# Explicit 4x4 inverses with TensorE sums, key dimension outermost, half roots and TensorE-made gated weights in a gated delta-rule block

## The chip, the cores and the metric

The kernel runs on one core of one Trainium2 chip. The metric is the time of one execution on the device, in microseconds (us), from the start of the program to its end. Everything is computed in float32.

## The reference

A block with adaptive layer norms: an attention part with a recurrent state (a gated delta rule), then a feed-forward part in which each row goes to one of 8 experts. The batch is 16, the length 256, the width 128, with 16 heads of 8 dimensions.

```python
h = _layernorm(x) * (1 + ca) + sa            # sa, ca, ga, sb, cb, gb from silu(c) @ wmod
q, k = silu(h @ Wq), silu(h @ Wk); v = h @ Wv            # per head, 8 dimensions
k = k * rsqrt(sum(k * k, -1) + 1e-12)
beta = 2.0 * sigmoid(h @ Wbet); a = sigmoid(h @ Wf)
def step(S, inp):                            # 256 steps, S is 8x8 for each batch row and head
    Sd = a * S
    u = v - einsum('bhk,bhkv->bhv', k, Sd)
    Sn = Sd + beta * k[..., None] * u[:, :, None, :]
    return Sn, einsum('bhk,bhkv->bhv', q, Sn)
o = o * rsqrt(mean(o * o, -1) + 1e-6)
x = x + ga * ((o.reshape(b, n, d) * norm_w) @ Wo)
h = _layernorm(x) * (1 + cb) + sb
x = x + gb * experts(h)                      # argmax of 8, silu(a) * g @ w2, times the top probability
```

## The kernel before, in words

The 128 partitions hold 8 batch rows times 16 heads, so the recurrence has two halves h = 0 and 1 (8 batch rows each). Time is cut into chunks of C = 4 steps: there are 64 chunks, n = 0 to 63. The first 128 steps (chunks 0 to 31) are slice 0, the others slice 1. A group g is four chunks.

Inside a chunk the four steps are coupled by a lower-triangular 4x4 matrix (tile L, one for each chunk, from the products of unit keys, decays and beta). Solving with it is forward substitution, `substitute(h, s, j)` for j = 0, 1, 2: a product of a column of L with a row of X (written to TMP), then a subtraction from the rows below it. VectorE does both. For slice 0 this is done ahead of the loop. For slice 1 it is done in the gaps of the loop.

VectorE runs the loop over the chunks. Each chunk has four steps for each half: `from_state` (L1476), `sum_u` (L1482), `outer` (L1489), `next_state` (L1495). After each of these eight instructions VectorE takes one piece of a second list of work, `next(other)`. That list is `second_preparation` (slice 1: key norms, unit keys, decay factors, key products, substitution), then `first_slice_rows` (gated output weights, sums of squares, roots, second layer norm and routing of slice 0). `after_chunk(n)` holds the list back until chunk n is done; the constants `PREP`, `SOLVE`, `AT_WOG`, `AT_ROOT` and so on are such chunks. `settle` gives up the turn after an instruction whose result is needed by the next piece.

ScalarE follows the same chunks with a fixed order written in a loop over n. In each round it first copies `ubar` (if n is even), scales the state (`decay`, L1060, which `next_state` of the same chunk waits for), stages keys every fourth chunk (`stage`), keeps states (`keep_states`, L1074), evacuates finished outputs from PSUM (`out_group`, L1090, at the chunks of `OUT_AT`), then does single jobs such as `query_evac` (L1028, at the chunks of `QK_AT`).

GpSimd makes the products of queries with states and of weights with U for each group and half (`make_products`, L280 and L287, into two alternating slots of prod_o), and in between the products of slice 1: `multiply_keys` (L833), `weigh_keys` (L799), `multiply_queries` (L824), `decay_keys` (L810), `decay_queries` (L841, L846). TensorE sums these products with an identity as weights and accumulates in PSUM: `sum_outputs` (L570, L574), `sum_queries` (L589), `sum_keys` (L602). `make_products` waits until the slot's last sum is done, and `sum_outputs` waits until the bank has been evacuated by `out_group`. For queries and keys the products lie with the key dimension k innermost (8 floats), so TensorE reads every eighth float.

A reciprocal root is made in three parts. VectorE adds the epsilon (L1347, L1306, L1504), ScalarE takes `Sqrt` (`root`, L944), and VectorE takes the reciprocal (L1354, L1287) and refines it by one Newton step.

The gated output weights WOG[b] = norm_w * Wo * gate[b] are made by TensorE and VectorE: TensorE spreads the gate of row b over the partitions (`gate_columns`, L557), then VectorE multiplies it by NW and WO (`weigh_columns`, L1449, sixteen instructions in chunks 32 to 35).

After the loop the last outputs are squared, summed, scaled (L239), moved by DMA, multiplied by WOG (`attend`, L618), and the feed-forward part follows: tiles of 128 rows, 46 of them, each on TensorE with the weights of one expert (L715, L730).

## Time and profile before

| | |
|---|---|
| median of 3 runs | 510.71 us (509.48 to 512.72) |
| the profiled execution | 512.15 us, of which 510.4 us are the span of the profile |
| busy in the span | PE 372.3, PEld 309.3, DVE 415.1, ACT 272.7, POOL 276.6 us |
| mean granted TensorE clock | 0.873 |

PE is TensorE's matmuls and PEld its weight loads, DVE is VectorE, ACT is ScalarE, POOL is GpSimd. The rows give the start of an instruction from the start of the span. An fp32 matmul stands as two records. In a row of the timeline, neighbouring instructions of one line are merged (x4), and the idle time in front of them stands in brackets with what ended it. The recorded durations of VectorE overlap a little: of two that follow each other directly, the second starts some 0.08 us before the first one's recorded end. What one costs the others is therefore the distance between starts.

### The profile page before, as it was taken

To read this page: it belongs to the slowest core of one execution; us is meant where nothing else is said; L and a number is where in the kernel's file an instruction comes from. 1 tells how busy PE (TensorE), PEld (TensorE's weight loads), DVE (VectorE), ACT (ScalarE), POOL (GpSimd) and SP (SyncE) were. 2 spreads that over 40 slices of the span, in tenths; PEclk is the share of its full clock that TensorE was granted. 3 is DMA by queue.
4 is the path that set the end of the run, shared out by engine and by line. 5 is a ranking of instruction groups with operands and counts; after the bars stand their busy time and mean duration, and the time that the engine had idled before them with its cause. 6 is when DMAs were issued, how large, how long until landed. Compare 5 with 4: busy or idle time off the path is not lost. (4 is left out here: it accounts for less than half of the span.)

```text
span 510.4 us, 8398 instructions
## 1 busy us (share of the span) xinstructions
PE 372.3 (73%) x2387; PEld 309.3 (61%) x2387; DVE 415.1 (81%) x1196; ACT 272.7 (53%) x600; POOL 276.6 (54%) x323
## 2 busy tenths in 40 slices
PE   2855861959928789843296876585999998999970
PEld 1312220426526658843296766585989997999970
DVE  4759999999999999999999899966595743559734
ACT  2587876957225225464556546273375566655520
POOL 1166244889999959641838828601132277633340
PEclk9996786888869799777598977799899999999995
DMA  8185788990000002910400000114313013424006
GB/s 218 45 89 98 89 115 131 141 71 2 0 0 2 0 0 81 368 49 0 75 10 2 0 1 32 54 36 76 76 39 105 31 54 105 130 59 133 29 26 170
DMA packets 50203, 34.98 MB, mean 69 GB/s; under 512 B 10992, under 2 KB 46608, under 8 KB 50032
## 3 DMA queue, kind: packets, MB, share of 16 engines
q1 hardware_dynamic: 47152, 29.07, 29.4%
q0 software_dynamic: 3008, 5.40, 3.5%
q8 instruction: 20, 0.33, 0.3%
q14 instruction: 23, 0.19, 0.2%
HBM read 15.26 MB, written 10.27 MB: 50 GB/s over the span
## 5 line engine op out<-in xcount | busy, mean ns | idle before, releaser
L570 PE MATMUL bank<-prod_o,ID 128*128 128x128 f32 x512 | 80.6, 323 | 43.1 <-POOL prod_o L287 21.7
L570 PEld LDWEIGHTS bank<-prod_o,ID 128*128 128x128 f32 x512 | 75.3, 233 | 48.0 <-POOL prod_o L287 24.6
L918 POOL DMA_INDIRECT placed_y<-Q,place x46 | 44.1, 958 | 98.6 <-ACT Q L1223 56.2
L715 PE MATMUL bank<-Q,p 128*128 128x128 f32 x736 | 95.0, 277 | 0.0
L715 PEld LDWEIGHTS bank<-Q,p 128*128 128x128 f32 x736 | 89.9, 193 | 0.1
L1060 ACT ACTIVATE p<-S,GAM 128x64 f32<-128x64 f32 x126 | 48.4, 409 | 75.9 <-DVE S L1495 75.2
L280 POOL TENSOR_TENSOR prod_o<-Q,ST 128x1024 f32<-128x1024 f32 x28 | 61.9, 2211 | 37.3 <-PE bank L574 26.2
L1216 ACT ACTIVATE p<-big 128x1024 f32 x46 | 48.5, 1057 | 44.3 <-PE bank L715 41.7
L1495 DVE TENSOR_REDUCE S<-p 128x64 f32<-128x320 f32 x126 | 55.1, 471 | 0.8 <-ACT p L1060 0.8
L1482 DVE TENSOR_REDUCE U<-p 128x32 f32<-128x288 f32 x128 | 52.4, 437 | 0.0
L1476 DVE TENSOR_TENSOR p<-S,bank 128x256 f32<-128x256 f32 x128 | 49.0, 405 | 0.7 <-ACT bank L1055 0.7
L1489 DVE TENSOR_TENSOR p<-U,bank 128x256 f32<-128x256 f32 x126 | 47.1, 405 | 0.0
L537 PE MATMUL bank<-ph,WP 128*128 128x512 f32 x48 | 32.1, 823 | 18.8 <-ACT ph L956 12.7
L287 POOL TENSOR_TENSOR prod_o<-PD,U 128x128 f32<-128x128 f32 (+1 forms) x112 | 42.5, 415 | 0.0
L865 POOL DMA_INDIRECT sorted_h<-X,pos x32 | 30.8, 964 | 14.1 <-issue 8.5
L1685 DVE COPY Q<-bank 128x128 f32<-128x128 f32 x46 | 13.2, 287 | 28.7 <-PE bank L703 28.6
L730 PE MATMUL bank<-big,S 128*128 x248 | 33.3, 277 | 2.0 <-DVE Q L1699 2.0
L574 PEld LDWEIGHTS bank<-prod_o,ID 128*128 128x128 f32 x256 | 34.3, 208 | 0.0
L574 PE MATMUL bank<-prod_o,ID 128*128 128x128 f32 (+3 forms) x256 | 33.8, 279 | 0.0
L1692 DVE TENSOR_TENSOR S<-S,bank 128x512 f32<-128x512 f32 x31 | 21.2, 685 | 15.4 <-PE bank L715 14.4
L730 PEld LDWEIGHTS bank<-big,S 128*128 128x128 f32 x248 | 30.1, 192 | 2.8 <-issue 2.8
L537 PEld LDWEIGHTS bank<-ph,WP 128*128 128x128 f32 x48 | 11.4, 254 | 33.0 <-issue 16.2
(225 smaller groups left out, 747.5 us busy)
## 6 DMA issues: line engine op xcount, KB each, us to landing
big<-in_L_ffn_w_dram SPq DMA_DIRECT2D x1, 4096.0 KB, 13.4
big<-big SPq DMA_DIRECT2D x16, 192.0 KB, 4.7
Q<-sorted_h SPq DMA_DIRECT2D x46, 64.5 KB, 2.1
sorted_h<-ZERO SPq DMA_DIRECT2D x2, 1472.0 KB, 16.3
X<-in_L_attn_x_dram SPq DMA_DIRECT2D x8, 256.0 KB, 4.5
big<-big SPq DMA_DIRECT2D x16, 128.0 KB, 5.1
X<-Q SPq DMA_DIRECT2D x32, 64.0 KB, 2.4
K<-placed_y SPq DMA_DIRECT2D x8, 256.0 KB, 3.5
```

The costliest lines, as they stand in the source:

```text
L280: engine.tensor_tensor(slot[:, 0:HD, :, :, :], q, states.unsqueeze(3).broadcast_to(full), ALU.mult)
L570: pe.matmul(ps, ID[:, :], prod_o[:, k % 2, i, :], start=(i == 0), stop=False, skip_group_check=True)
L574: m = pe.matmul(o4, ID[:, :], r4, start=False, stop=(d == C - 1), skip_group_check=True)
L715: m = pe.matmul(bank[(1, 6)[g % 2] + k][:, c * P:(c + 1) * P], W1E[g % 2][:, f:f + P], XST[:, g % 3, :], start=True, stop=True)
L730: m = pe.matmul(bank[3][:, 0:D], GU[g % 3][:, c * P:(c + 1) * P], W2[:, bass.ds(expert, 1), c, :], start=(c == 0), stop=(c == FC - 1))
L918: pool.indirect_dma_start(placed_y[g // NF], bass.IndirectOffsetOnAxis(ap=place[:, g:g + 1], axis=0), YS[:, g % YR, :], None).then_inc(sem ...
L1060: act.activation(p2[h][:, :, :, C], S_[h][:, n % SR, :, :], ACT.Copy, scale=GAM[h][:, n:n + 1])\
L1216: act.activation(W1E[g % 2].unsqueeze(1), W1[:, bass.ds(expert, 1), :], ACT.Copy).then_inc(sem("w1_copied"), 1)
L1476: dve.tensor_tensor(p1[h][:, n % UR, :, :, 0:HD], s_, w, ALU.mult).then_inc(sem("seq_w", h), 1)
L1482: dve.tensor_reduce(U_[h][:, n % VR, :, :], p1[h][:, n % UR, :, :, :], AX_X, ALU.add)\
L1489: dve.tensor_tensor(p2[h][:, :, :, 0:C], u, k, ALU.mult).then_inc(sem("state_in", h), 1)
L1495: dve.tensor_reduce(S_[h][:, (n + 1) % SR, :, :], p2[h][:, :, :, :], AX_X, ALU.add).then_inc(sem("s_ready", h), 1)
```

## The change

It has five parts.

- Slice 1, half 0: the three pairs of product and subtraction are replaced by `invert(0)` (six small VectorE instructions that turn L into the inverse's entries) and `multiply_solved(0)` (the three products with the untouched X, without subtractions). TensorE sums row i and its i products in bank 0 (`solve(0, i)`), ScalarE copies the sum back to X (`solved(0, i)`, at chunks 19, 23 and 24 for i = 3, 2, 1). Half 1 is still solved by substitution.
- The products of queries and keys lie with k outermost: GpSimd writes with a step of 320 or 192 floats between neighbouring k, and TensorE reads contiguous columns.
- Roots: ScalarE takes `Abs_reciprocal_sqrt` of 4x + 4 eps, so it gives half of the reciprocal root, and VectorE does three instructions. The epsilon instruction, the reciprocal and (for the keys) a copy are gone. The operands of two of the three are now both in SBUF also for the keys. An early `Sqrt` of ScalarE after the loop is gone.
- Gated weights: TensorE transposes Wo and the gates once (`turn_weights`), ScalarE makes sixteen diagonal matrices (two in each of chunks 15 to 22, `spread_gates`), TensorE multiplies (`weigh_columns`, 16 matmuls in front of group 6), and ScalarE scales by norm_w while it copies (`scale_columns`, chunks 31 to 34). VectorE's sixteen instructions are gone.
- `OUT_AT` of group 4 goes from chunks 25, 25 to 26, 27, and of group 5 from 27, 28 to 28, 29. In TensorE's order, `solve(0, 3)` stands after the sums of group 2, and `solve(0, 2)` and `solve(0, 1)` after those of group 3, in front of the last `sum_queries`. Some waits are moved to other semaphores.

```diff
+    SOLVED = (C, 2)
+    SOLVE_AT = {(2, 1): (3,), (3, 1): (2, 1)}
+    SOLVED_AT = {19: 3, 23: 2, 24: 1}
-    OUT_AT = {..., 4: (25, 25), 5: (27, 28), 6: (30, 31), ...
+    OUT_AT = {..., 4: (26, 27), 5: (28, 29), 6: (30, 31), ...
...
+        def by_dimension(region, pairs):
+            return region[:, 0:pairs * HD].rearrange("p (k x) -> p k x", k=HD)
-                    m = pe.matmul(..., ID[:, :], terms[:, :, k], ...)
+                    m = pe.matmul(..., ID[:, :], query_terms(j)[:, k, :], ...)
...
+            def solve(h, i):
+                if i == C - 1:
+                    pe.wait_ge(sem("solved_terms"), h + 1)
+                else:
+                    pe.wait_ge(sem("prep_done", h), C - 1 - i + 1)
+                pe.matmul(solved_sum(h), ID[:, :], solved_row(h, i), start=True, stop=False)
+                for j in range(i):
+                    m = pe.matmul(solved_sum(h), ID[:, :], solved_products(h, j)[:, :, i - j - 1, :], ...)
+                m.then_inc(sem("solved_ps"), 1)
+            def weigh_columns():
...
+                    m = pe.matmul(bank[(5, 0, 1, 4)[b // 4]][...], WO[:, :], WOG[:, b, :], start=True, stop=True)
...
                     sum_outputs(g, h)
+                    for i in SOLVE_AT.get((g, h), ()):
+                        solve(0, i)
...
-                act.activation(dst, src, ACT.Sqrt).then_inc(sem("root_out"), 1)
+                act.activation(half, src, ACT.Abs_reciprocal_sqrt, scale=4.0, bias=4.0 * eps).then_inc(sem("root_out"), 1)
...
+            def solved(h, i):
+                act.wait_ge(sem("solved_ps"), (C - 1) * h + C - i)
+                act.activation(solved_row(h, i), solved_sum(h), ACT.Copy).then_inc(sem("prep_done", h), 1)
...
-            act.activation(sd[:, :], ve[:, :], ACT.Sqrt)
...
-                yield from settle(dve.reciprocal(y, sroot))
-                yield from settle(dve.tensor_tensor(t, y, y, ALU.mult))
-                yield from settle(dve.scalar_tensor_tensor(out=t, in0=t, scalar=-0.5, in1=var, op0=ALU.mult, op1=ALU.mult))
-                dve.scalar_tensor_tensor(out=y, in0=t, scalar=1.5, in1=y, op0=ALU.add, op1=ALU.mult)...
+                yield from settle(dve.scalar_tensor_tensor(out=t, in0=half, scalar=-4.0, in1=half, op0=ALU.mult, op1=ALU.mult))
+                yield from settle(dve.scalar_tensor_tensor(out=t, in0=var, scalar=eps, in1=t, op0=ALU.add, op1=ALU.mult))
+                dve.scalar_tensor_tensor(out=y, in0=t, scalar=3.0, in1=half, op0=ALU.add, op1=ALU.mult)...
...
+            def invert(h):
+                yield from settle(dve.tensor_tensor(two, pair(2, 1, 2), pair(1, 0, 2), ALU.mult))
+                yield from settle(dve.tensor_tensor(one, pair(3, 1), pair(1, 0), ALU.mult))
+                yield from settle(dve.tensor_tensor(pair(2, 0, 2), pair(2, 0, 2), two, ALU.add))
+                yield from settle(dve.tensor_tensor(other_, pair(3, 2), pair(2, 0), ALU.mult))
+                yield from settle(dve.tensor_tensor(one, one, other_, ALU.add))
+                yield from settle(dve.tensor_tensor(pair(3, 0), pair(3, 0), one, ALU.add))
+            def multiply_solved(h):
+                for j in range(C - 1):
...
+                    last = dve.tensor_tensor(solved_products(h, j), col..., X4[:, :, j:j + 1, :]..., ALU.mult)
...
             def second_preparation():
...
-                yield from substitute(0, 1, 0)
+                yield from invert(0)
+                yield from multiply_solved(0)
                 yield from unit_keys(1, 1)
                 yield
-                for j in (1, 2):
-                    yield from substitute(0, 1, j)
             def first_slice_rows():
-                for q in range(4):
-                    yield from after_chunk(AT_WOG + q)
-                    yield from weigh_columns(q)
```

## Rows read from the trace of the kernel before

**Rows 1.** Page, part 1: busy time, share of the span, instructions.

```profile
PE 372.3 (73%) x2387; PEld 309.3 (61%) x2387; DVE 415.1 (81%) x1196; ACT 272.7 (53%) x600; POOL 276.6 (54%) x323
```

**Rows 2.** Windows: busy time of PE, PEld, DVE, ACT, POOL in a stretch, granted clock.

```profile
129.00:149.00 20.00, 13.71 (x63) 8.67 (x61) 20.00 (x31) 3.66 (x14) 19.84 (x21) 0.84 0.00 0
```

**Rows 3.** Waits of VectorE: waited for, us in total, times, longest.

```profile
DVE sm L1415 <- PE bank L602: 0.6, 1, 0.6
```

**Rows 4.** Timeline of VectorE, chunks 30 and 31, first step: start, us.

```profile
205.35 0.73 DVE L1476 TENSOR_TENSOR p<-S,bank 128x256 f32<-128x256 f32 x2
...
208.18 0.73 DVE L1476 TENSOR_TENSOR p<-S,bank 128x256 f32<-128x256 f32 x2
```

**Rows 5.** Timeline of VectorE, chunk 32, the first of sixteen.

```profile
211.33 0.33 DVE L1449 SCALAR_TENSOR_TENSOR ph<-bank,NW,WO 128x128 f32<-128x128 f32 x1
211.60 0.40 DVE L1476 TENSOR_TENSOR p<-S,bank 128x256 f32<-128x256 f32 x1
```

**Rows 6.** Groups of instructions: busy us, mean ns of one.

```profile
L1287 DVE RECIPROCAL sm<-sm 128x256 f32<-128x256 f32 x2 | 3.5, 1745 | 0.0
```

**Rows 7.** Timeline of VectorE: the root of slice 1's second half of keys.

```profile
136.15 0.95 DVE L1354 RECIPROCAL bank<-bank 128x128 f32<-128x128 f32 x1
137.01 0.39 DVE L1482 TENSOR_REDUCE U<-p 128x32 f32<-128x288 f32 x1
137.32 0.27 DVE L1355 COPY XN<-bank 128x128 f32<-128x128 f32 x1
137.51 0.40 DVE L1489 TENSOR_TENSOR p<-U,bank 128x256 f32<-128x256 f32 x1
```

**Rows 8.** Groups by shape, VectorE, 120 to 226 us: slice 1's substitution, both halves.

```profile
L1431 DVE TENSOR_TENSOR big<-big,X 128x1536 f32<-128x1536 f32 x2 | 5.5, 2768 | 0.0
L1433 DVE TENSOR_TENSOR X<-X,big 128x1536 f32<-128x1536 f32 x2 | 5.5, 2732 | 0.0
...
L1431 DVE TENSOR_TENSOR big<-big,X 128x512 f32<-128x512 f32 x2 | 4.6, 2276 | 0.0
L1431 DVE TENSOR_TENSOR big<-big,X 128x1024 f32<-128x1024 f32 x2 | 2.6, 1315 | 0.0
L1433 DVE TENSOR_TENSOR X<-X,big 128x1024 f32<-128x1024 f32 x2 | 2.5, 1254 | 0.0
...
L1433 DVE TENSOR_TENSOR X<-X,big 128x512 f32<-128x512 f32 x2 | 1.7, 840 | 0.0
```

**Rows 9.** Timeline of VectorE: one product ahead of the loop and in it.

```profile
75.07 1.76 DVE L1431 TENSOR_TENSOR big<-big,X 128x1536 f32<-128x1536 f32 x1
...
130.05 3.62 DVE L1431 TENSOR_TENSOR big<-big,X 128x1536 f32<-128x1536 f32 x1
```

**Rows 10.** Timeline of GpSimd beside the second of them.

```profile
129.89 2.16 POOL L280 TENSOR_TENSOR prod_o<-Q,ST 128x1024 f32<-128x1024 f32 x1
```

**Rows 11.** Timeline of VectorE ahead of the loop: first substitution of half 0.

```profile
51.76 1.76 DVE L1431 TENSOR_TENSOR big<-big,X 128x1536 f32<-128x1536 f32 x1 [0.82 <-POOL X L799]
```

**Rows 12.** Timeline of TensorE: last sum of queries, first sum of group 4.

```profile
176.36 9.43 PE L589 MATMUL bank<-big,ID 128*128 128x320 f32 x16
187.22 2.02 PE L570 MATMUL bank<-prod_o,ID 128*128 128x128 f32 x16 [1.44 <-ACT K L1090]
```

**Rows 13.** Timeline of ScalarE: outputs of group 3 (chunk 23), group 6 (chunk 30).

```profile
186.77 0.46 ACT L1090 ACTIVATE K<-bank 128x128 f32<-128x128 f32 x2
...
207.80 0.28 ACT L1090 ACTIVATE K<-bank 128x128 f32<-128x128 f32 x1 [0.94 <-PE bank L574]
```

**Rows 14.** Single lines of GpSimd: min/median/max ns.

```profile
L239 POOL TENSOR_TENSOR Q<-K,sm x2: 2848/2849/2850, 241.7 to 244.5; 128x1024 f32<-128x1024 f32 x2
...
L841 POOL TENSOR_TENSOR Q<-Q,XN x2: 1972/1975/1978, 105.4 to 196.7; 128x1024 f32<-128x1024 f32 x2
```

**Rows 15.** Groups: GpSimd's query products of three of the four blocks.

```profile
L824 POOL TENSOR_TENSOR big<-Q,K 128x1024 f32<-128x1024 f32 (+3 forms) x12 | 18.1, 1536 | 0.8 <-DMA XN<-ph 0.8
```

**Rows 16.** Timeline of TensorE: the first attend of slice 1.

```profile
355.61 2.93 PE L618 MATMUL bank<-ph,X 128*128 128x128 f32 x16 [2.55 <-DMA X<-Q]
```

More of the change, by code:

```diff
@@ L363, in key_pairs, with solved_products, solved_row, solved_sum @@
             return tiles
+        def solved_products(h, j):
+            at = SCH * 2 * HD * sum(C - 1 - i for i in range(j))
+            m = C - 1 - j
+            return big[:, 3072 * h + at:3072 * h + at + SCH * m * 2 * HD].rearrange("p (n i x) -> p n i x", n=SCH, i=m)
+        def solved_row(h, i):
+            return slice_rows(X_[h], 1).rearrange("p (n i) x -> p n i x", i=C)[:, :, i, :]
+        def solved_sum(h):
+            return bank[h][:, 0:SCH * 2 * HD].rearrange("p (n x) -> p n x", n=SCH)
         def query_rows(j, d):
@@ L663, in _ @@
                 sum_queries(j)
+            turn_weights()
             for g in range(NG):
@@ L1002, in _ @@
             evacuate(1)
-            root(sd[:, :], ve[:, :])
+            root(yy[:, :], mv[:, :, 1], LN_EPS)
             shift(2)
@@ L1439, in substitute, with pair @@
                     dve.wait_ge(sem("prep_done", h), s + 1)
-            def weigh_columns(q):
-                if q == 0:
-                    dve.wait_ge(sem("wo_in"), 16 * 4)
-                    landed(dve, 1, 1)
-                    dve.wait_ge(sem("staged"), 2 * NHALF * NG // 2)
-                dve.wait_ge(sem("ga_ps"), q + 1)
-                for b in range(4 * q, 4 * q + 4):
-                    dve.scalar_tensor_tensor(out=WOG[:, b, :], in0=bank[(5, 0, 1, 4)[q]][:, b % 4 * D:(b % 4 + 1) * D], scalar=NW[:, 0:1],
-                                             in1=WO[:, :], op0=ALU.mult, op1=ALU.mult).then_inc(sem("wog_ready"), 1)
+            def invert(h):
+                def pair(i, j, count=1):
+                    first = C * i + j
+                    return L[:, :, first:first + (count - 1) * (C + 1) + 1:C + 1]
+                t_ = slice_vectors(h, 1)[5]
+                two = t_[:, 0:2 * SCH].rearrange("p (n e) -> p n e", n=SCH)
+                one = t_[:, 2 * SCH:3 * SCH].unsqueeze(2)
+                other_ = t_[:, 3 * SCH:4 * SCH].unsqueeze(2)
+                yield from settle(dve.tensor_tensor(two, pair(2, 1, 2), pair(1, 0, 2), ALU.mult))
[5 more added lines that the diff above has]
+            def multiply_solved(h):
+                dve.wait_ge(sem("uw_started", h), 4)
+                dve.wait_ge(sem("q_raw", h), 2)
+                X4 = slice_rows(X_[h], 1).rearrange("p (n i) d -> p n i d", i=C)
+                for j in range(C - 1):
+                    full = [P, SCH, C - 1 - j, 2 * HD]
+                    col = L[:, :, C * (j + 1) + j:C * C:C]
+                    last = dve.tensor_tensor(solved_products(h, j), col.unsqueeze(3).broadcast_to(full),
+                                             X4[:, :, j:j + 1, :].broadcast_to(full), ALU.mult)
+                    if j == C - 2:
+                        last.then_inc(sem("solved_terms"), 1)
                     yield
@@ L1637, in first_slice_rows @@
                 yield from after_chunk(AT_ROOT)
-                yield from rsqrt(*(sm[:, i, :] for i in (2, 3, 4, 5)))
+                yield from rsqrt(sm[:, 2, :], O_EPS, sm[:, 4, :], sm[:, 4, :], sm[:, 5, :])
                 for i, n in enumerate(AT_STATS):
@@ L1737, in _ @@
                 if g == 0:
-                    now(rsqrt(*(sm[:, i, :] for i in (2, 3, 4, 5))))
+                    now(rsqrt(sm[:, 2, :], O_EPS, sm[:, 4, :], sm[:, 4, :], sm[:, 5, :]))
                 if g - 1 in F_ATTEND:
```

149 lines of the change are left out of this document (86 added, 63 removed).

## The prediction

> **What bounds the kernel now.** I read the page first: VectorE is busy for 415 us of 510, the most of all engines [rows 1]. Then the windows: in the loop, for instance from 129 to 149 us, VectorE is busy for 20.00 of 20 us, ScalarE for 3.7, and GpSimd for 19.84 [rows 2]. So up to chunk 63 the end is set by VectorE's own instructions, with GpSimd full beside it in this part. The waits of VectorE inside the loop are small; the one that concerns this change is 0.6 us for the sums of the keys [rows 3]. A chunk without other work takes 208.18 - 205.35 = 2.83 us [rows 4]. Behind the loop there is a chain: last root, scaling, DMA, attend, in front of which TensorE stands idle for 2.6 us [rows 16]; whatever shortens this chain or the loop moves the rest forward, and behind it TensorE is the engine that is full. So an instruction taken from VectorE's list is worth its distance between starts, provided that nothing becomes later than the loop.
>
> **The change part by part.** The sum is made against the profiled execution, 512.15 us, which is 1.44 above the median of 510.71; I take the same difference off both.
>
> *Gated weights.* One of VectorE's instructions costs 211.60 - 211.33 = 0.27 us [rows 5]; sixteen make 4.3 us. In their place ScalarE gets sixteen 128x128 and four 128x512 copies in chunks 15 to 22 and 31 to 34, some 1 us in a chunk of 2.83, and is mostly idle there [rows 2]. Gain 4.3.
>
> *Roots of 256 columns.* The reciprocal takes 1.745 us, 1.66 between starts, and the epsilon instruction some 0.2 to 0.3 [rows 6, 7]. The three other instructions stay three. One such root lies in the loop (gain 1.9), the other in the chain in front of attend (gain 1.75, as VectorE must still wait for the tile that it copies in between). The missing early `Sqrt` lets ScalarE load its table later, beside VectorE's last sum: zero; without that cover it would be about 1 us.
>
> *Small roots of the layer norms.* At the start of the kernel, and in the loop, epsilon and a short reciprocal go: about 0.5 and 0.7 us. The one at the second layer norm of slice 1 lies beside TensorE's tiles: zero.
>
> *Ahead of the loop, keys.* Each of the two roots loses about 1.6 us on VectorE. For half 0 that is wasted: the first substitution already waits 0.82 us for GpSimd's weighted keys [rows 11], and these follow ScalarE and GpSimd, not VectorE, so more wait takes its place. For half 1 up to 2 us could be gained, but see the next point. I count 0 (0 to 2); the 0.5 of the layer norm above is what passes through.
>
> *Two inputs in SBUF.* The product of 1536 columns takes 1.76 us ahead of the loop and 3.62 us at 130.05 [rows 9]. GpSimd had started one of its products at 129.89, for 2.16 us [rows 10]: VectorE's instruction ended 1.6 us after that one's end, so it did no work until then. Instructions with an operand in PSUM show nothing of the kind: the copies of the root beside a full GpSimd take 0.27 us [rows 7]. The change puts more instructions under this condition: six of `invert` and two of each root of keys, which had operands in PSUM. The Trainium skill (SBUF - State Buffer, Who interferes with whom) says the same: a VectorE instruction with two SBUF inputs contends with a GpSimd instruction that reads SBUF, and the second to start blocks until the first is done. By that rule, the trace agrees; without it this change would be worth some 8 to 10 us more than my sum.
>
> A long GpSimd product (2.1 us) is followed by four short ones. A blocking instruction that comes in a long one loses 1 to 2 us, in a short one 0.1 to 0.2. *Roots of slice 1's keys*, two of them: before, each cost 137.01 - 136.15 = 0.86 for the reciprocal, four times 0.19 for the others [rows 7], and 0.2 for epsilon: 1.8 us. After: three times 0.2, and one long block, 1.5: 2.1 us. Together a loss of 0.5 (gain of 2.5 without any block, loss of 3 with a block each time).
>
> *Half 0's solution.* Before, both halves sum up to 5.5 + 5.5 + 4.6 + 2.6 + 2.5 + 1.7 = 22.4 us [rows 8]; half of it, less six overlaps of 0.08, is 10.7 us. After: the products alone, 1.7 + 1.15 + 0.6 = 3.45 unblocked, and six small ones of 0.12, together 4.2 us. For the nine blocking instructions I count three long blocks (two in `invert`, one in the products) and the rest short: 5.0 us. That gives 9.2, a gain of 1.5 (6.5 with no block, a loss of 2 with five long ones).
>
> *Key dimension outermost.* TensorE's sum of 8 times 320 columns takes 9.43 us for 16 records, 1.84 ns a column, where 16 times 128 contiguous columns take 2.02, 0.99 ns a column [rows 12]. So I expect about 5.1 us for the sum of queries, and the sums of keys in proportion. On VectorE this takes away the 0.6 us wait [rows 3]. GpSimd's writes get a large step; no row shows such a write. Between its products of 1024 columns the trace has 1.97 us (contiguous) and 2.85 (one input with a step of 8 floats) [rows 14]. Taken as bounds: no extra, or 44% on the queries' 6.0 us a block [rows 15] and on the keys. I take no extra as likeliest, since in the nearest row it is a read that is strided. The Trainium skill (GPSIMD Engine Reference, Performance pitfalls for Q7 kernels) states the penalty for reads with a step above 8 bytes, and no penalty for writes; but SBUF - State Buffer (Door 1) has lines of 16 bytes, each crossing of which is paid, and by that the upper bound would hold.
>
> *The new wait in TensorE's queue.* `solve(0, 1)` waits for ScalarE's copy of row 2, at chunk 23 behind the outputs of group 3, which are out at 187.2 in before's time [rows 13]. The copy takes 0.6: 187.8. Queued behind it in order are the last sum of queries and all outputs from group 4 on. Before, that sum was done long ahead (at 185.8), and group 4 began at 187.22, right after the evacuation [rows 12]. Now: 187.8 + 2.0 (two sums of 512 columns, each two records) + 5.1 = 194.9, or 7.7 us later. From there on TensorE (2.7 a half), GpSimd (3.3 a half) and the 16 gate matmuls, which stand in front of group 6 as before, have little slack: group 6 was evacuated at 207.80 with ScalarE already waiting 0.94 for TensorE [rows 13]. About 2 us of the 7.7 are regained from small gaps. ScalarE stands in `out_group` for group 6 (chunks 30, 31, unchanged) until about 213.1, and then makes the state scaling that VectorE needs 2.0 us into chunk 31, at 210.2: VectorE waits 3.4, and about 1.1 more one chunk later, behind the second half of group 6. From group 8 on, its outputs are asked for much later, and all is caught up. Loss 4.5. From below: 0, if gaps absorb more. From above: 10, if contiguous reading didn't help (9.4 instead of 5.1).
>
> *Sum.* 4.3 + 1.9 + 1.75 + 0.5 + 0.7 + 0 - 0.5 + 1.5 + 0.6 - 4.5 = 6.25. That gives 505.9 for the profiled execution and 504.5 for the median.
>
> **The rivals.**
> *Blocks hardly bite and VectorE gets all of its savings.* The blocks cost 8 us in my sum (3.0 at the roots, 5.0 at the solution), and 2 more ahead of the loop. Without them the gain is 16, and 494.5 us; with the wait of TensorE's queue gone as well, 490. For it: relative times of the two engines shift, and short GpSimd instructions let VectorE in. Against it: GpSimd has 19.84 of 20 us filled in just this stretch [rows 2].
> *TensorE's and GpSimd's chain becomes the bound (the slower side).* If strided writes cost 44%, the two blocks of slice 0 and the first keys bring GpSimd 7 us behind ahead of chunk 12, of which 3 come back through TensorE's faster sum: VectorE waits 4 instead of saving 0.6. Behind it the rest of the lag and the wait in the queue make up 10 instead of 4.5 at group 6. The sum is 6.25 - 4.6 - 5.5 = -3.9, or 514.6; with long blocks twice as often, 517. It decides from a penalty of about 25%, where the gain is used up.
> *The change does less than it says.* VectorE's own time falls by the 10 us, and stalls for ScalarE and blocks give all of it back: 509 to 512. For it: ScalarE's waits for TensorE are there already [rows 13].
>
> **How the numbers follow.** My forecast 504.5 has a chance of 0.42 with its own range of 500 to 508.5. The faster rival has 0.24 (488 to 499), the balance 0.18, the slower rival 0.16 (513 to 518). The range that leaves out no more than 2 in 10 is 493 to 515. A measurement here tells about 1%: 505.6 and 515.8. Faster: the faster rival and some 0.27 of my forecast, 0.51. Slower: the worse part of the slower rival, 0.10. The same: 0.39.
>
> **What the profile will show.** Busy time of VectorE falls by about 17 us plus or minus the blocks. Sums of queries take 5 us for 16 records, not 9.4; if 9.4, the stride was not their cost. GpSimd's query products stay at 1.54 us on average; 2.0 or more means the slower rival. VectorE's rows of `invert` have a few of 1 to 2 us among ones of 0.2: blocks. Waits of `next_state` for ScalarE's scaled state sum up to 4 to 5 us in chunks 30 to 33, and ScalarE waits for TensorE in front of them. If neither is there, I am wrong on the side of too little gain; if ScalarE waits from chunk 25 on, on the side of too much.

## The result and the profile after

Measured: 506.66 us (median of 8, 505.34 to 508.02) against 511.51 for the kernel before (median of 8). The ratio is 0.9904, with a 95% interval of 0.9883 to 0.9925: 0.5 to 1.2% faster, 4.85 us. The profiled execution took 507.04 us with a span of 505.2, against 510.4 before, so 5.2 us separate the two traces. The page of the changed kernel, busy time by engine (the kernel before has its own in [rows 1]):

```profile
PE 363.4 (72%) x2407; PEld 313.7 (62%) x2407; DVE 404.8 (80%) x1159; ACT 278.6 (55%) x624; POOL 273.4 (54%) x323
```

VectorE is busy for 10.3 us less, but only half of that reaches the end. To find where it goes, read on VectorE's timeline when `from_state` of a chunk starts, in both traces. The distance between the two columns is what has been gained so far:

| start of chunk, us | before | changed | gained since the row above |
|---|---|---|---|
| 0 | 83.52 | 80.79 | 2.73 |
| 7 | 109.93 | 107.72 | -0.52 |
| 12 | 125.40 | 122.99 | 0.20 |
| 13 | 129.72 | 126.64 | 0.67 |
| 17 | 156.99 | 153.53 | 0.38 |
| 26 | 194.03 | 190.12 | 0.45 |
| 36 | 226.46 | 226.33 | -3.78 |
| 40 | 242.96 | 240.91 | 1.92 |
| 49 | 274.05 | 270.99 | 1.01 |
| 62 | 324.54 | 321.89 | -0.41 |
| `attend` of slice 1 | 355.61 | 350.78 | 2.18 |

`from_state` is L1476 before and L1570 now. One stretch gives back nearly all that had come before it: chunks 26 to 36. The waits of VectorE in it, on its timeline (in brackets how long it stood idle, and for whom):

```profile
194.62 0.88 DVE L1589 TENSOR_REDUCE S<-p 128x64 f32<-128x320 f32 x2 [2.38 <-ACT p L1110]
206.44 0.88 DVE L1589 TENSOR_REDUCE S<-p 128x64 f32<-128x320 f32 x2 [0.42 <-ACT p L1110]
212.40 0.88 DVE L1589 TENSOR_REDUCE S<-p 128x64 f32<-128x320 f32 x2 [3.04 <-ACT p L1110]
216.64 0.88 DVE L1589 TENSOR_REDUCE S<-p 128x64 f32<-128x320 f32 x2 [1.32 <-ACT p L1110]
222.71 0.88 DVE L1589 TENSOR_REDUCE S<-p 128x64 f32<-128x320 f32 x2 [0.31 <-ACT p L1110]
```

L1589 is `next_state`, L1110 ScalarE's scaling of the state. Together 7.47 us. ScalarE in turn stood in front of sums that TensorE had not made: first of the last queries' (L1078, `query_evac` in chunk 25, in front of the wait of 2.38 in chunk 26), then of outputs (L1140, `out_group`, in front of the other four, 5.09 together):

```profile
193.26 0.66 ACT L1078 ACTIVATE PD<-bank 128x128 f32<-128x128 f32 x4 [4.45 <-PE bank L625]
...
202.17 0.28 ACT L1140 ACTIVATE K<-bank 128x128 f32<-128x128 f32 x1 [2.42 <-PE bank L611]
205.43 0.28 ACT L1140 ACTIVATE K<-bank 128x128 f32<-128x128 f32 x1 [2.44 <-PE bank L611]
211.80 0.28 ACT L1140 ACTIVATE K<-bank 128x128 f32<-128x128 f32 x1 [4.16 <-PE bank L611]
```

And TensorE's own timeline shows the root of it, an idle stretch of 9.20 us at `solve(0, 1)` (L646), with the last sum of queries (L625) and group 4 (L607) queued behind it:

```profile
183.86 2.08 PE L646 MATMUL bank<-X,ID 128*128 128x512 f32 x2 [9.20 <-ACT X L1203]
185.73 1.92 PE L648 MATMUL bank<-big,ID 128*128 128x512 f32 x2
187.44 5.79 PE L625 MATMUL bank<-big,ID 128*128 128x320 f32 x16
193.06 1.95 PE L607 MATMUL bank<-prod_o,ID 128*128 128x128 f32 x16
```

Group 4 had begun at 187.22 before [rows 12]. From the outputs on, the chain is the one that was forecast: the waits of chunks 30 to 32 are 0.42, 3.04 and 1.32 us, 4.78 together. The 2.38 of chunk 26, by way of the queries, comes on top.

The inverse, on VectorE's timeline, and GpSimd's products beside it (a single name behind the arrow stands for both inputs; `bank` is PSUM, all others here are SBUF):

```profile
126.96 1.22 DVE L1526 TENSOR_TENSOR sm<-big 128x64 f32<-128x64 f32 x1
128.44 1.81 DVE L1527 TENSOR_TENSOR sm<-big 128x32 f32<-128x32 f32 x1
130.54 0.45 DVE L1528 TENSOR_TENSOR big<-big,sm 128x64 f32<-128x64 f32 x1
131.23 0.20 DVE L1529 TENSOR_TENSOR sm<-big 128x32 f32<-128x32 f32 x1
131.69 1.80 DVE L1530 TENSOR_TENSOR sm<-sm 128x32 f32<-128x32 f32 x1
133.74 0.20 DVE L1531 TENSOR_TENSOR big<-big,sm 128x32 f32<-128x32 f32 x1
```

```profile
126.09 1.97 POOL L859 TENSOR_TENSOR K<-K,sm 128x1024 f32<-128x1024 f32 x1
128.02 2.17 POOL L283 TENSOR_TENSOR prod_o<-Q,ST 128x1024 f32<-128x1024 f32 x1
130.15 1.20 POOL L290 TENSOR_TENSOR prod_o<-PD,U 128x128 f32<-128x128 f32 x4
131.31 2.12 POOL L283 TENSOR_TENSOR prod_o<-Q,ST 128x1024 f32<-128x1024 f32 x1
```

Read an end on one engine against an end on the other: GpSimd's first instruction ends at 128.06 and L1526 at 128.18, its second at 130.19 and L1527 at 130.25, its fourth at 133.43 and L1530 at 133.49. Three instructions of 32 or 64 columns ended just after what GpSimd had running. Those that started beside its short ones (L290) took 0.20 and 0.45.

### The profile page after: what moved, and what is told of

Same layout as the page of the kernel before. It is cut to its first block, busy times and chain, and to the rows that moved or that the text cites. A ratio compares the mean times of both kernels' runs of the same rounds, so it can differ in the third digit from the quotient of the medians.

```text
span 505.2 us, 8431 instructions
## 1 busy us (share of the span) xinstructions
PE 363.4 (72%) x2407; PEld 313.7 (62%) x2407; DVE 404.8 (80%) x1159; ACT 278.6 (55%) x624; POOL 273.4 (54%) x323
## 4 chain that ended last, share of the span: by engine, by line
DVE 44%; PE 28%; issue 12%; POOL 6%; DMA 4%; ACT 3%; SPq 2%; ACTq 0%; POOLq 0%; DVEq 0%
PE bank L764 11%; DVE U L1576 6%; DVE S L1589 5%; PE bank L779 5%; DVE p L1570 5%; DVE p L1583 5%; PE bank L607 4%; DVE big L1506 3%; DVE X L1508 2%; PE bank L611 2%; DVE K L1433 2%; POOL prod_o L283 1%; POOL placed_y L968 1%; DVE big L1473 1%; PE bank L692 1%
## 5 line engine op out<-in xcount | busy, mean ns | idle before, releaser
L607 PE MATMUL bank<-prod_o,ID 128*128 128x128 f32 x512 | 79.1, 318 | 45.7 <-POOL prod_o L290 25.7
L607 PEld LDWEIGHTS bank<-prod_o,ID 128*128 128x128 f32 x512 | 73.5, 228 | 47.8 <-POOL prod_o L290 26.9
L1110 ACT ACTIVATE p<-S,GAM 128x64 f32<-128x64 f32 x126 | 46.8, 409 | 58.6 <-DVE S L1589 58.1
L1589 DVE TENSOR_REDUCE S<-p 128x64 f32<-128x320 f32 x126 | 55.3, 473 | 8.3 <-ACT p L1110 8.3
L1570 DVE TENSOR_TENSOR p<-S,bank 128x256 f32<-128x256 f32 x128 | 49.1, 408 | 0.7 <-ACT bank L1105 0.7
L566 PE MATMUL bank<-ph,WP 128*128 128x512 f32 x48 | 31.8, 816 | 17.4 <-ACT ph L1007 13.4
L290 POOL TENSOR_TENSOR prod_o<-PD,U 128x128 f32<-128x128 f32 (+1 forms) x112 | 38.6, 382 | 0.0
L611 PE MATMUL bank<-prod_o,ID 128*128 128x128 f32 (+3 forms) x256 | 35.8, 289 | 0.0
```

Of the source, the lines that this page charges most:

```text
L607: pe.matmul(ps, ID[:, :], prod_o[:, k % 2, i, :], start=(i == 0), stop=False, skip_group_check=True)
L611: m = pe.matmul(o4, ID[:, :], r4, start=False, stop=(d == C - 1), skip_group_check=True)
L1110: act.activation(p2[h][:, :, :, C], S_[h][:, n % SR, :, :], ACT.Copy, scale=GAM[h][:, n:n + 1])\
L1570: dve.tensor_tensor(p1[h][:, n % UR, :, :, 0:HD], s_, w, ALU.mult).then_inc(sem("seq_w", h), 1)
L1589: dve.tensor_reduce(S_[h][:, (n + 1) % SR, :, :], p2[h][:, :, :, :], AX_X, ALU.add).then_inc(sem("s_ready", h), 1)
```

## The experiments

They ran on two chips. On the first the kernel before took 511.91 us (copy_earlier, half0_substituted, dimension_innermost and before_half_roots), on the second 539.15 and 537.88 (the other eight runs). The loop takes about as long on both: in the changed kernel's two traces chunk 62 starts at 321.89 and 322.42, in copy_earlier's two at 314.10 and 315.28. The additional 26 to 30 us lie behind it. So ratios are taken on one chip, and traces are compared by their starts in the loop, where a difference of 1 us between two of them says nothing yet. These starts, in us:

| chunk | before | changed | copy_earlier | half0_subst. | dim._innermost | before_half_roots | inverse_in_psum | roots_in_psum | all_in_psum |
|---|---|---|---|---|---|---|---|---|---|
| 0 | 83.52 | 80.79 | 80.78 | 80.83 | 80.61 | 81.31 | 81.38 | 80.32 | 80.54 |
| 4 | 96.17 | 93.38 | 93.35 | 93.42 | 93.19 | 93.89 | 93.96 | 92.91 | 93.12 |
| 7 | 109.93 | 107.72 | 107.68 | 107.77 | 107.56 | 109.33 | 108.30 | 105.72 | 106.07 |
| 13 | 129.72 | 126.64 | 126.60 | 126.69 | 127.69 | 128.91 | 127.40 | 124.64 | 125.16 |
| 17 | 156.99 | 153.53 | 153.51 | 155.38 | 154.58 | 156.95 | 147.94 | 150.54 | 144.79 |
| 22 | 177.25 | 173.39 | 173.82 | 173.68 | 179.03 | 175.40 | 167.76 | 170.62 | 163.26 |
| 26 | 194.03 | 190.12 | 190.38 | 191.88 | 193.82 | 193.64 | 184.32 | 187.37 | 181.16 |
| 31 | 208.18 | 207.24 | 204.51 | 206.01 | 214.35 | 207.77 | 198.47 | 201.52 | 195.30 |
| 36 | 226.46 | 226.33 | 218.65 | 220.46 | 233.03 | 226.04 | 215.51 | 216.20 | 209.67 |
| 62 | 324.54 | 321.89 | 314.10 | 317.28 | 328.42 | 321.74 | 311.11 | 311.75 | 305.12 |

**copy_earlier: the wait in TensorE's queue.** The theory: `solve(0, 1)` stands waiting for ScalarE's copy, everything behind it is late, and ScalarE passes that on to VectorE. The rival: TensorE and GpSimd simply have too much to do.

```
-    SOLVED_AT = {19: 3, 23: 2, 24: 1}
+    SOLVED_AT = {19: 3, 22: 2, 23: 1}
```

> The changed kernel with the two last row copies of half 0 one chunk earlier on ScalarE (rows 2 and 1 in chunks 22 and 23 instead of 23 and 24); nothing else. Theory A, the wait in TensorE's queue: in the changed kernel TensorE stood idle for 9.20 us (174.7 to 183.9) at solve(0, 1), and everything queued behind it is late by that. Here solve(0, 1) starts at about 176 and the sum of queries is done at about 183 instead of 193; the new waits of next_state for the scaled state, 7.5 us in chunks 26 to 34, fall to 2 or less: 500 to 502 us. Rival B, the load itself: TensorE (six more 512-column sums, sixteen 128-column gate products) and GpSimd cannot keep up whatever the order, the waits stay at 5 us or more, 505 to 507 us.

500.49 us, ratio 0.9769 (0.9721 to 0.9817). TensorE's timeline, to be laid beside the one above:

```profile
174.25 1.12 PE L646 MATMUL bank<-X,ID 128*128 128x512 f32 x2 [0.69 <-ACT X L1203]
175.21 1.02 PE L648 MATMUL bank<-big,ID 128*128 128x512 f32 x2
176.07 4.47 PE L625 MATMUL bank<-big,ID 128*128 128x320 f32 x16
183.58 3.59 PE L607 MATMUL bank<-prod_o,ID 128*128 128x128 f32 x16 [3.04 <-ACT K L1140]
```

Group 4 starts 9.5 us earlier, chunks 26 to 36 take 28.27 us instead of 36.21, and none of the five waits is left. Two copies moved by one chunk give 6.2 us, more than the whole change had. The rival is out: the load is the same, and so is GpSimd's.

**outputs_later: the second link.** The same wait, relieved at ScalarE's end instead.

```
-    ... 4: (26, 27), 5: (28, 29), 6: (30, 31), 7: (33, 34),
+    ... 4: (28, 29), 5: (30, 31), 6: (33, 34), 7: (35, 35),
```

> The changed kernel with ScalarE taking out groups 4 to 7 later (chunks 28/29, 30/31, 33/34, 35/35 instead of 26/27, 28/29, 30/31, 33/34); TensorE's queue is left as it is, with its wait for the row copy. Theory A (second link: it is ScalarE, standing in program order in front of an output that is not there, that is late with the scaled state): TensorE is as late as before with group 4 (193), but nobody asks for it before it is there; the waits of next_state fall from 7.5 to 2 or 3 us: 501 to 503 us on the chip where the changed kernel takes 506.7. Rival (TensorE itself, or GpSimd's products, are what VectorE waits for through another way): no change, 506 to 507, or slower, since the later copies hold TensorE's two banks.

530.63 us on the second chip, ratio 0.9846 (0.9806 to 0.9886), where the changed kernel has 0.9966. The waits of `next_state` sum up to 2.6 us in its list of waits (8.3 in the changed kernel's, one old wait of 0.8 in either). The four in chunks 30 to 34 are gone, and one of 0.60 in chunk 36 is new. TensorE is later than in the changed kernel (group 4 starts at 196.61, in changed_again at 193.74), and it hardly matters, since ScalarE doesn't stand in line for it. So it is the order of ScalarE's list that carries TensorE's lag to VectorE. Two things blur the run. The first wait is still there (1.26 in chunk 26), as the edit doesn't touch `query_evac`; it is shorter because VectorE itself came to chunk 26 later, at 194.77 instead of 190.82 in changed_again, after an instruction that took 7.91 us (below). And the profiled execution, 534.86 us, is the slowest of four. Chunks 26 to 36 take 29.61 us instead of 36.18.

**half0_substituted: what the inverse is worth.** The inverse, its products and the row copies go; half 0 is substituted again as in the kernel before.

```
-    SOLVED = (C, 2) ... SOLVE_AT = {(2, 1): (3,), (3, 1): (2, 1)} ... SOLVED_AT = {19: 3, 23: 2, 24: 1}
+    SOLVED = (2, 2) ... SOLVE_AT = {} ... SOLVED_AT = {}
...
-                yield from invert(0)
-                yield from multiply_solved(0)
+                yield from substitute(0, 1, 0)
                 yield from unit_keys(1, 1)
                 yield
+                for j in (1, 2):
+                    yield from substitute(0, 1, j)
```

> The changed kernel with half 0 of the second slice solved by forward substitution again, as before the change (no inverse, no products by TensorE, no row copies); roots, key dimension outermost and gated weights stay. Theory A (queue): the 7.5 us of new waits go, the solution costs VectorE 10.7 us instead of 10.4: 499 to 501 us, so the inverse as placed is a loss. Rival B: the new waits come from the gated weights and GpSimd and stay, and VectorE's own time grows by 0.3 to 2: 507 to 509 us. Rival C: the inverse saves VectorE what it would without any block, 6.5 us, in this execution: 510 us or more, less what waits it takes along.

503.22 us, ratio 0.9802 (0.9734 to 0.9869; its four times spread from 499.5 to 505.5). In this kernel the factors of half 0 kept the sign that the inverse wants, so the second slice's first half was solved with the wrong sign; the instructions are those of the substitution. The new waits are gone but for 0.2 us, as the theory says. Against copy_earlier, which has lost them too, chunks 13 to 17 take 28.69 us instead of 26.91: the inverse saves 1.8 us of VectorE's time. Set against the 7.47 us of waits that it brought where the change had put its copies, it was a loss. I repeated it on the second chip with the right sign:

```
-                if s == 1 and h == 0 and d == 1:
-                    yield from settle(dve.scalar_tensor_tensor(out=w, in0=at(beta, 1, C), scalar=-1.0, ...))
-                else:
-                    yield from settle(dve.tensor_tensor(w, ...))
+                yield from settle(dve.tensor_tensor(w, ...))
```

> half0_substituted with its factors of half 0 taken with their right sign (that run had kept the inverse's sign, so its output lacked only that); the times must agree with it: 500 to 504 us. Against copy_earlier this says what the inverse gives once it holds up no queue: forecast 1.5 us by the prediction's term; copy_earlier's trace against half0_substituted's says 1.8.

531.33 us, ratio 0.9867 (0.9835 to 0.9898). The times that I had expected hold for the first chip; what compares is the ratio, which lies in the other run's interval. Chunks 13 to 17 take 28.69 us again. copy_earlier on the same chip (below) has 529.37, and 26.90 for these chunks. So the 1.8 us in chunks 13 to 17 are shown twice; what of it reaches the end is less sure: 2.0 us here and 2.7 on the first chip, with intervals that overlap, and 1.3 and 3.2 at the start of chunk 62.

**dimension_innermost: the stride.** The layout of the terms alone, back to what it was.

```
-            return region[:, 0:pairs * HD].rearrange("p (k x) -> p k x", k=HD)
+            return region[:, 0:pairs * HD].rearrange("p (x k) -> p k x", k=HD)
```

> The changed kernel with the terms of all sums of queries and keys laid out again with the key dimension innermost, both for GpSimd's writes and TensorE's reads. Theory A (TensorE's stride): the sum of 8 times 320 columns takes 9.4 us again instead of 4.5 to 5.8 at the same clock, GpSimd's query products stay at 6.05 us a block (so the large step of its writes cost nothing), the wait for the keys' sums of about 0.6 comes back, and group 4 is later by 3.6 to 4.9, which adds 3 to 5 us of waits of next_state: 510 to 512 us. Rival B (hidden): only the 0.6 comes back: 507 to 507.5 us.

513.87 us, ratio 1.0032 (1.0000 to 1.0063), 7 us above the changed kernel. TensorE's sum of queries, in the same place as above:

```profile
190.96 9.37 PE L625 MATMUL bank<-big,ID 128*128 128x320 f32 x16
```

GpSimd's four query products take 6.04 to 6.06 us here, with a contiguous write, and 6.05 to 6.09 in the changed kernel, with the large step. Of the 6.70 us at chunk 36, 3.0 are longer waits of `next_state` (11.3 instead of 8.3 in its list of waits), 1.0 was there at chunk 13, the wait for the keys' sums. The rest, 2.7, lies in half 1's substitution, whose six instructions take 13.4 us together instead of 10.8. One of them took 7.90, and the five others 3.5 less than in the changed kernel. On VectorE's timeline, and GpSimd's beside it:

```profile
169.15 7.90 DVE L1506 TENSOR_TENSOR big<-big,X 128x1536 f32<-128x1536 f32 x1
```

```profile
169.07 2.13 POOL L283 TENSOR_TENSOR prod_o<-Q,ST 128x1024 f32<-128x1024 f32 x1
171.16 1.20 POOL L290 TENSOR_TENSOR prod_o<-PD,U 128x128 f32<-128x128 f32 x4
172.33 2.13 POOL L283 TENSOR_TENSOR prod_o<-Q,ST 128x1024 f32<-128x1024 f32 x1
174.42 2.74 POOL L290 TENSOR_TENSOR prod_o<-PD,U 128x128 f32<-128x128 f32 x4
```

The same instruction took 1.74 in the changed kernel. Counted back by that from its end at 177.05, it began to work at 175.3: it had been held through nine GpSimd instructions in a row (one long, four short, one long, three short), which had no gap between them. The tenth, of 32 columns, then took 1.80 us instead of 0.25: now GpSimd was held. outputs_later shows the same (7.91 us at 170.10) with the new layout, so it isn't the stride's doing in itself; that this execution had it and the changed kernel's two had not I put down to when the two engines meet, which no run tried. In the trace the layout's own cost is 1.0 and 3.0 us of waits. How many of the ten executions, which took 510.5 to 516.2 us, had the long hold isn't known, so the 7 us of the medians can't be split in this way.

The sum with the old layout hardly depends on the clock: 9.37 us at a granted clock of 1.00, 9.53 at 125.82 with a mean of 0.82. Contiguous reading takes 4.47 at 1.00 (copy_earlier), 5.79 at a mean of 0.77 and 7.56 at 0.60 (at 126.00 in the changed kernel). What the new layout gives is therefore largest where the clock is full.

**before_half_roots: one part alone.** `Abs_reciprocal_sqrt` and its three instructions, in the kernel before.

```
-                act.activation(dst, src, ACT.Sqrt).then_inc(sem("root_out"), 1)
+                act.activation(half, src, ACT.Abs_reciprocal_sqrt, scale=4.0, bias=4.0 * eps).then_inc(sem("root_out"), 1)
-                yield from settle(dve.reciprocal(rn, rt))
-                yield from settle(dve.tensor_copy(d2, rn))
... 
+                yield from rsqrt(n2, K_EPS, d2, rn, t_)
```

> The kernel before with the half roots alone (Abs_reciprocal_sqrt on ScalarE, no reciprocal and no epsilon instruction on VectorE, mean of squares scaled on ScalarE). By the terms of the prediction: 0.5 at the start, 0 at the keys' roots ahead of the loop, -0.5 at those of slice 1, 1.9 and 0.7 in the loop, 1.75 behind it: 4.35 faster, ratio 0.991, chunk 0 starts at 83.0. Rival (the front follows ScalarE and TensorE, which are both earlier, and TensorE is granted its full clock between 40 and 47 us, where the kernel before has half): chunk 0 starts at 80.8 as in the changed kernel, 6 to 7 us faster in all, ratio 0.987. If chunk 0 starts at 80.8 with the clock at half, the roots themselves gave it.

505.86 us, ratio 0.9848 (0.9794 to 0.9902), 6 us faster; by the two traces 3.9 us (span 506.5), as the profiled execution, 508.30, is the slowest of four. Chunk 0 starts at 81.31, so 2.2 of the changed kernel's 2.73 us at the front come with this part, where I had 0.5. The keys' roots of slice 1 cost more here than before: chunks 4 to 7 take 15.44 us instead of 13.76, chunks 13 to 17 28.04 instead of 27.27. That is 2.45 us lost where I had forecast 0.5; in the changed kernel the first of them lost 0.6. Which instructions are held depends on what GpSimd has running at that moment.

**Operands in PSUM.** If two inputs in SBUF are what lets GpSimd hold VectorE, one of them in PSUM must end it, at the same work. The base is copy_earlier, so that no queue covers the effect. roots_in_psum puts the temporary of the keys' roots there and swaps the two products:

```
+                yield from settle(dve.scalar_tensor_tensor(out=t, in0=var, scalar=eps, in1=half, op0=ALU.add, op1=ALU.mult))
+                yield from settle(dve.scalar_tensor_tensor(out=t, in0=t, scalar=-4.0, in1=half, op0=ALU.mult, op1=ALU.mult))
...
-                yield from rsqrt(n2, K_EPS, d2, rn, t_)
+                yield from key_rsqrt(n2, K_EPS, d2, rn, rt)
```

> The earlier copies (as in copy_earlier), and the temporary of the four keys' roots in PSUM with the two products reordered, so that each of the three instructions has one input in PSUM; same count. Theory A: the three instructions take 0.3 each everywhere; they took 1.06, 0.27 and 1.17 at 93.7 to 96.7, 0.28, 0.27 and 1.30 at 140.5 to 142.9 and up to 1.62 ahead of the loop at 58.7 in the changed kernel: gain 0.8 + 0.9 + 0.9 to 1.0 + up to 1.3, 2.7 to 4 us: 496.5 to 498 us. Rival B: the block moves on to the next instruction with two SBUF inputs or no effect of the operand at all: 500 to 501.

inverse_in_psum keeps the factors in a free bank and one diagonal also in SBUF, so that each instruction has one input in either memory:

```
+        LP = bank[0][:, 0:SCH * C * (C - 1)].rearrange("p (n a) -> p n a", n=SCH)
+                    yield from settle(dve.tensor_copy(L[:, :, C:C * C:C + 1], diag))
...
-                yield from settle(dve.tensor_tensor(two, pair(2, 1, 2), pair(1, 0, 2), ALU.mult))
+                yield from settle(dve.tensor_tensor(two, pair(2, 1, 2), copy(1, 0, 2), ALU.mult))
...
-                    col = L[:, :, C * (j + 1) + j:C * C:C]
+                    col = LP[:, :, C * j + j:C * (C - 1):C]
```

> The earlier copies (as in copy_earlier), and the factors of half 0 of the second slice (its L, the inverse, one temporary) in PSUM, with a copy of one diagonal in SBUF, so that none of the nine instructions of inverse and products has two inputs in SBUF; one small instruction more. Theory A (a VectorE instruction with two SBUF inputs is held while GpSimd runs one of its products): the inverse's six take 0.2 to 0.3 each and the products 1.8, 1.2 and 0.7; between the starts of chunks 13 and 14 it is about 5 us less than the 12.44 of copy_earlier, all of it kept: 495 to 496 us. Rival B (GpSimd and VectorE share bandwidth whatever the operand, or the wait is for something else): no change, 500 to 501, plus 0.2.

all_in_psum has both, and half 1's factors in bank 1 in the same way (`LP[h]`, and `col` of `substitute` from it). As bank 1 is then in use, the gate matmuls wait until half 1 is solved.

> inverse_in_psum and roots_in_psum together, and the factors of half 1 of the second slice in PSUM too, so that its three products are unblocked as well (its three subtractions keep two inputs in SBUF). Theory A: the gains add (5 + 3), and the products of half 1, which were held once for 1.5 us (at 176.88 in the changed kernel), gain 0 to 2 more: 490 to 493 us. Rival B: 500 to 501. Rival C (something else becomes the bound, TensorE or GpSimd, since VectorE is now 8 us earlier): waits of next_state for the scaled state in chunks 26 to 34 give back half: 495 to 497.

Ratios on the second chip: 0.9760 (0.9724 to 0.9796) for the roots, 0.9722 (0.9691 to 0.9753) for the inverse, 0.9634 (0.9605 to 0.9664) for all; copy_earlier has 0.9834 there (below). These are some 4, 6 and 11 us, the size that theory A gave, and no interval touches copy_earlier's (0.9800 to 0.9868). The same six instructions of the inverse, with the same products on GpSimd, in inverse_in_psum:

```profile
127.72 0.26 DVE L1534 TENSOR_TENSOR sm<-bank,big 128x64 f32<-128x64 f32 x1
128.23 0.20 DVE L1535 TENSOR_TENSOR sm<-bank,big 128x32 f32<-128x32 f32 x1
128.71 0.22 DVE L1536 TENSOR_TENSOR bank<-bank,sm 128x64 f32<-128x64 f32 x1
129.20 0.20 DVE L1537 TENSOR_TENSOR bank<-big,bank 128x32 f32<-128x32 f32 x1
129.64 0.18 DVE L1538 TENSOR_TENSOR sm<-bank,sm 128x32 f32<-128x32 f32 x1
130.07 0.19 DVE L1539 TENSOR_TENSOR bank<-bank,sm 128x32 f32<-128x32 f32 x1
```

```profile
126.71 1.97 POOL L861 TENSOR_TENSOR K<-K,sm 128x1024 f32<-128x1024 f32 x1
128.64 2.13 POOL L283 TENSOR_TENSOR prod_o<-Q,ST 128x1024 f32<-128x1024 f32 x1
```

Six instructions take 1.25 us instead of the changed kernel's 5.68, and chunk 13 takes 6.35 instead of copy_earlier's 12.44. In roots_in_psum chunks 4 to 7 take 12.81 instead of 14.33, chunks 13 to 17 25.90 instead of 26.91. The rival (bandwidth shared whatever the operand) is out. The Trainium skill (SBUF - State Buffer, Who interferes with whom) says that an instruction of VectorE with one SBUF input at most, outside its two-port modes, doesn't contend with GpSimd, and that one with two does when GpSimd reads SBUF; the traces agree, with 0.20 and 1.81 us for the same 32 columns. Not all of it is kept to the end of the loop: in inverse_in_psum chunks 26 to 36 take 31.19 us instead of 28.27, of which 2.6 are waits for ScalarE's scaled state, with ScalarE again in front of groups 5 to 7. Chunk 62 starts 3.0 us earlier there than in copy_earlier's first trace and 4.2 earlier than in its second, 2.4 and 3.5 in roots_in_psum, and 9.0 and 10.2 in all_in_psum, where those chunks take 28.51. Why the waits return in one and not in the other I haven't settled; the two differ in when VectorE and GpSimd hold each other in chunks 20 to 23.

**The same chip for all.** The changed kernel and the two that beat it, again:

> The changed kernel itself, for a comparison on the same chip: ratio to the kernel before 0.990, as measured.

> copy_earlier itself, on the same chip as all_in_psum: ratio to the kernel before 0.977, 6 us below changed_again; the same waits gone.

> all_in_psum itself on the same chip as the kernels that it is to be compared with. Theory A (two SBUF inputs): 8 to 10.5 us below copy_earlier_again (the starts of chunk 62 in the two traces that exist, 314.10 and 305.12, are 9.0 apart), ratio 0.958 to 0.962 on a chip where the kernel before takes 511. Rival B (what the loop gains is lost behind it, where TensorE is full): 3 to 5 us below.

| kernel | us | ratio to before (537.88) | 95% |
|---|---|---|---|
| changed_again | 536.12 | 0.9966 | 0.9937 to 0.9994 |
| copy_earlier_again | 529.37 | 0.9834 | 0.9800 to 0.9868 |
| all_in_psum_again | 519.01 | 0.9644 | 0.9612 to 0.9675 |

6.75 us between the first two and 10.4 between the last two (10.7 by the starts of chunk 62): both steps are confirmed. The ratios that I had expected for the first two, 0.990 and 0.977, did not come on this chip; the distances did. all_in_psum is the best version that I have: 17 us under the changed kernel at the same arithmetic.

## Why the prediction was right, and where it wasn't

504.5 was forecast, 506.66 measured: inside the range. That is 0.95% under the kernel before, so it counts as the same by the prediction's 1%, which had 0.39 where faster had 0.51. The sum was 6.25, the result 4.85 (5.2 by the traces). That they lie so near is in part luck: the gain ahead of the loop was 2.2 larger than its term, the loss at TensorE's queue 3.0 and the solution of half 0 1.2 worse than theirs. VectorE's busy time fell by 10.3 us, where 17 plus or minus the blocks was meant. The terms:

*Gated weights, 4.3.* Right. Chunks 31 to 38 take 25.05 us in before_half_roots, which has VectorE's sixteen, and 20.92 in copy_earlier, 21.47 in its second trace: 4.1 and 3.6. In the changed kernel itself they can't be seen, as waits fill their place.

*Roots of 256 columns, 1.9 and 1.75.* Right: 1.92 over chunks 36 to 40, and 2.18 between chunk 62 and `attend`. The small root in the loop, with its epsilon, gave 1.0 instead of 0.7.

*Ahead of the loop, 0.5.* The largest miss upwards: 2.73. The layer norms' roots gave the 0.5 to 0.6 (0.32 at the first, 0.3 at the second). The rest shows in three places. First, TensorE: its first six 512-column products took 5.46 us before and 4.37 after (from 16.60 and 16.28; the granted clock reads 1.00 in both, so the record doesn't say why). Second, half 0's keys: from the start of their sum of squares to that of the product with the root it is 1.4 less (2.87 instead of 4.26), of which 1.2 went again, as three products of keys were held by GpSimd (4.23 instead of 3.04). Third, the wait of 0.82 for GpSimd's weighted keys [rows 11], which I had taken to grow, was gone. GpSimd's `weigh_keys` is queued behind its gate moves, these wait for the fourth block's evacuation, and that came 4.7 us earlier (42.06 instead of 46.79). 1.9 us of that are an earlier start and 2.65 a shorter run of six products on TensorE. They stand second here, below the six of the block ahead, in the kernel before, and then in the changed one:

```profile
30.80 2.84 PE L537 MATMUL bank<-ph,WP 128*128 128x512 f32 x6 [3.01 <-ACT ph L956]
...
40.11 5.46 PE L537 MATMUL bank<-ph,WP 128*128 128x512 f32 x6 [4.90 <-ACT big L966]
```

```profile
29.38 4.54 PE L566 MATMUL bank<-ph,WP 128*128 128x512 f32 x6 [3.01 <-ACT ph L1007]
...
38.23 2.81 PE L566 MATMUL bank<-ph,WP 128*128 128x512 f32 x6 [2.75 <-ACT big L1017]
```

The kernel before was granted 0.50 (1.2 GHz) from 39 to 46 us, after 4.90 us of idle time, and 1.00 (2.4 GHz) in the block ahead; the changed kernel had 0.50 in the block ahead, from 30 to 33 us, and 1.00 from 38 to 46 us, after 2.75 us of idle time. What that is worth two other traces tell. inverse_in_psum and outputs_later have the half roots, 1.00 in the block ahead, 4.3 us of idle time and 0.50 from 39 to 42 us. Their chunk 0 starts at 81.38 and 81.78, and their wait for the weighted keys is gone as well. In the eleven traces with half roots and 1.00 there it starts at 80.30 to 81.47. So with the clock against them the half roots still give 1.7 to 2.1 of the 2.73 us; the rest, up to 1, may be the clock's, but the eleven differ by as much. Why the stretch of 0.50 fell on the one block or the other was not tried. The step that failed is "I count 0 (0 to 2)": it took the weighted keys to be out of the roots' reach, while half 0's roots, ScalarE's evacuations and so GpSimd all came earlier.

*Slice 1's keys' roots, -0.5 together.* By the prediction's own prices it is -0.6 (twice 1.8 less 2.1), and -3.6, not -3, with two long blocks in each. For the first, -0.25 was meant and -0.52 came (chunks 0 to 7).

*Half 0's solution, +1.5.* The mechanism was right, the blocks were counted too low: three long ones in the inverse instead of two and one in the products (2.81 instead of 1.2). The nine instructions take 10.4 us, less their overlaps, where 9.2 was forecast and substitution had taken 10.7: a gain of 0.3. Chunks 13 to 17, which hold the second root too, gained 0.38 against the kernel before; against substitution with the same roots (half0_substituted) 1.8.

*Keys' sums, 0.6.* Right: 0.67 in chunk 12, and 1.0 is lost again with the old layout. *The stride.* Right: 4.47 us at full clock, 5.79 where the clock was granted at 0.50 at first, 9.37 with the old layout. GpSimd's writes with the large step cost nothing (6.05 to 6.09 us for four query products against 6.03 to 6.06), so the upper bound of 44%, which the prediction had from lines of 16 bytes, does not hold for them, and the slower rival lost its condition.

*The new wait in TensorE's queue, -4.5.* The right mechanism, place and order; the size was off. 7.47 us came. Those that were forecast for chunks 30 to 33 came as forecast, 4.78 us. The other 2.7 were missing from the term, 2.38 of them in chunk 26. I had sums of 512 columns at 1.0 us and the queries at 5.1, together 7.1 us from the copy to group 4; it took 9.20 (183.86 to 193.06), as TensorE, in its 9.20 us of idle time, had fallen to 0.50, and stayed there until 190.1. By these 2.1 us the last sum of queries came too late for ScalarE's `query_evac` in chunk 25, and VectorE stood in chunk 26: the case that the prediction had named as the sign of too much gain. That `query_evac` also stands in that queue's way, the term had left out. What I missed most is that the term could be had back: I treated the copy's chunk as given, while its sum had been there since 174.7.

*The rivals.* "Blocks hardly bite" was wrong as to this kernel, and its 490 would have been the worth of their absence: all_in_psum, without the queue's wait and most blocks, is 3.2% under the changed kernel, which would be 490.5 us on the first chip (506.66 x 519.01 / 536.12), an estimate. The balance ("the change does less than it says") came near in its way: five more us of VectorE's time were won than reached the end.

## What to carry to other kernels

When a step is put into the middle of an engine's list, look for when its input is ready and place the consumer there; one chunk too late cost more than the step saved. An instruction beside a busy GpSimd is priced by where its operands lie: with two inputs in SBUF a 0.2 us instruction takes up to 2, or as long as GpSimd's row without a gap lasts, and with one in PSUM it takes 0.2. Compare by the start of each stage in two traces: the 4.8 us at the end here are rows of +9.5 and -4.7 in the first table, and the gated weights' 4 us can't be seen in them at all.

## What was not expected of the hardware

- A VectorE instruction was held through nine GpSimd instructions, 7.9 us for 1.74 (in two traces). In the kernel before the longest that I had read was 3.6 [rows 9]. By the Trainium skill's page named above the second to issue waits until the first is done; these two rows say that it can go on through those that follow without a gap.
- The two chips differ by 5% in the same kernel (511.91 and 537.88). In the second's traces several waits of 4 to 11 us, with no releaser inside the core ("remote"), lie behind the loop; the first has none. From changed_again's list of waits (total, times, longest):

```profile
ACT S L1287 <- remote: 12.5, 2, 8.4
ACT p L1300 <- remote: 9.2, 1, 9.2
DVE S L1782 <- remote: 8.9, 1, 8.9
```

What they are is open; no run was made for it.
- The changed kernel's ratio is 0.9904 where the kernel before takes 511.51 us and 0.9966 where it takes 537.88, with intervals that don't touch: the gain of a change is not the same share everywhere. The kernel before has no trace on the second chip, so where the difference lies is open.
